# All three stages of a fused block written out without loops, and a layer's weights split partly one step early

## What is computed

```
x = x + ga * attention(norm(x), 16 heads of 8)                 # phase A, one sequence per item
h = norm(x); for i in range(6):                                # phase B, local attention, DEPTH = 6
    h = attn_layer(shift_tokens(h), Wqkv[i], ..., Wo[i]) + h   #   16 heads of 64, windows of 32 tokens
    h = ffn_layer(shift_tokens(h), ..., W1[i], W2[i]) + h      #   341 wide, gated by gelu
x = x + gb * h
x = x + ga * state_space(norm(x))                              # phase C, scan over the tokens
x = x + gb * (norm(x) @ W + low rank part)
```

## Time and profile before

| what | value |
|---|---|
| three timed runs | 4804.89, 4807.92 (median), 4809.58 us |
| the profiled execution | 4799.15 us |
| its span, first to last instruction | 4797.3 us |
| PE busy | 4226.0 us, 88% of the span |
| PE weight loads | 3150.4 us, 66% |
| DVE busy | 4007.1 us, 84% |
| ACT busy | 3749.9 us, 78% |
| POOL busy | 3518.3 us, 73% |
| phase A, about | 60 to 484 us |
| phase B, about | 484 to 4030 us |
| phase C, about | 4030 to 4797 us |
| mean granted clock of TensorE | 0.961 of 2.4 GHz |

### The profile page before, as it was taken

One profiled execution on the slowest core, in us unless ns is written; L12 is line 12 of the kernel. 1 busy time (PEld: TensorE's weight loads), 2 busy tenths in 40 slices (PEclk: granted clock), 3 DMA queues, 4 the chain that ended last, 5 costly groups with the idle time before them and its releaser, 6 DMA issues. The chain is left out here.

```text
span 4797.3 us, 131407 instructions
## 1 busy us (share of the span) xinstructions
PE 4226.0 (88%) x45166; PEld 3150.4 (66%) x45166; DVE 4007.1 (84%) x7658; ACT 3749.9 (78%) x11543; POOL 3518.3 (73%) x2504
## 2 busy tenths in 40 slices
PE   6988699998999989998889989999899998688887
PEld 3555477776777777776777767777677776354553
DVE  4776798888888888888888888898898895688887
ACT  2555588888888888888888888888888887677774
POOL 0100699988899888998989989899899995344444
PEclk9999799999999999999999999999999999788888
DMA  1000111111111111111111111111121111000000
GB/s 27 6 5 2 49 48 44 44 38 52 53 40 43 48 48 47 44 44 45 46 53 43 40 45 52 47 44 44 45 53 38 44 44 28 3 4 3 3 3 5
DMA packets 118641, 169.38 MB, mean 35 GB/s; under 512 B 26563, under 2 KB 44422, under 8 KB 118022
## 3 DMA queue, kind: packets, MB, share of 16 engines
q1 hardware_dynamic: 109246, 160.92, 12.7%
q10 hardware_dynamic: 8776, 0.45, 0.1%
HBM read 20.79 MB, written 2.10 MB: 5 GB/s over the span
## 5 line engine op out<-in xcount | busy, mean ns | idle before, releaser
L1377 POOL TENSOR_TENSOR b_w<-b_w,b_vt 128x512 f32<-128x512 f32 x768 | 1188.4, 1558 | 331.8 <-DVE b_vt L1289 184.1
L1381 POOL TENSOR_TENSOR b_rn<-b_ssm,all_neg_half 128x16 f32<-128x16 f32 x384 | 1171.7, 3051 | 32.0
L1174 ACT ACTIVATE b_Pr<-ps,b_nm 128x96 f32<-128x96 f32 x3072 | 1002.8, 353 | 3.4 <-DVE b_nm L1346 2.8
L1174 ACT ACTIVATION_READ_ACCUMULATOR b_Pr<-ps,b_nm 128x1 f32 x3072 | 677.1, 220 | 0.0
L1216 ACT ACTIVATE b_PT<-ps 96x512 f32<-96x512 f32 x768 | 458.1, 597 | 264.1 <-PE ps L1026 257.1
L1060 PE MATMUL ps<-b_Whi,b_xlo 128*128 128x512 f32 x1152 | 579.2, 503 | 61.7 <-DVE b_Wlo L1306 25.8
L989 PE MATMUL ps<-all_ident,b_w 128*128 128x128 f32 x3072 | 460.6, 281 | 182.3 <-DVE b_xtok L282 118.7
L1340 DVE TENSOR_TENSOR b_Pr<-b_Pr,b_rinv 128x384 f32<-128x384 f32 x768 | 547.0, 712 | 26.3
L1026 PE MATMUL ps<-all_ident,b_Pr 128*96 128x128 f32 x3072 | 479.2, 279 | 68.8 <-ACT b_PT L1216 47.1
L1287 DVE TENSOR_TENSOR b_w<-ps,until_b_rotab 128x512 f32<-128x512 f32 x768 | 524.0, 682 | 8.9 <-ACT b_sq L1193 5.4
L1346 DVE TENSOR_REDUCE b_nm<-ps 128x8 f32<-128x768 f32 x384 | 367.5, 957 | 190.8 <-PE ps L1015 184.6
(11 more groups left out here) (259 smaller groups left out, 9375.4 us busy)
## 6 DMA issues: line engine op xcount, KB each, us to landing
b_V<-b_Vraw SPq DMA_DIRECT2D x384, 192.0 KB, 2.6
b_V<-b_Vraw SPq DMA_DIRECT2D x384, 128.0 KB, 2.4
b_V<-b_Vraw SPq DMA_DIRECT2D x192, 64.0 KB
b_Wraw<-in_L_ffn_Wqkv SPq DMA_DIRECT2D x36, 256.0 KB, 3.4
b_Wo<-in_L_ffn_Wo SPq DMA_DIRECT2D x6, 512.0 KB, 4.5
a_xtok<-in_L_attn_hidden_states SPq DMA_DIRECT2D x16, 128.0 KB, 2.1
out<-c_xout SPq DMA_DIRECT2D x16, 128.0 KB, 1.8
b_W<-in_L_ffn_W SPq DMA_DIRECT2D x6, 341.0 KB, 3.3
```

Source lines behind the costliest of these rows:

```text
L1174: last = nc.scalar.activation(s.Pr[:, r % 2, j, i], ps[:, S_BANK[j], i * KEYS:(i + 1) * KEYS], ACT.Exp, bias=s.nm[:, r, j, i:i + 1], accum ...
L1377: nc.gpsimd.tensor_tensor(rows, rows, s.vt[:, i % 4], ALU.add).then_inc(s.pool_add, 1)
L1381: nc.gpsimd.tensor_tensor(s.rn[:, j], s.ssm[:, j], g.neg_half[:, 0:HB], ALU.pow).then_inc(s.pool_r, 1)
```

## The change

All steps of the three phases are written out with numbers; the three loops of the compute engines go. (SP keeps its own loops over the loads of phase A and the stores of phase C.) Since in phase B every step now knows its number, the step ahead of a layer's start can be told from the others (`last`): in it conversions 0 and 1 of the next layer are done, in slots 11 and 14, once the last pieces that read these columns are through. The `convert` step does the other four, in slots 1, 4, 7 and 10. At the very start (n = -1) conversions 0 and 1 stay in slot 0. The order of the last two chunks is swapped. SP's program for the loads of the raw weights isn't edited. The last two parts of the diff are ACT's and DVE's.

```
 def phase_a_steps(engine, body):
-    def whole(n):
+    for n in range(-2, NB + 2):
         body(StepA(n, n % 2, *[0 <= n + d < NB for d in (2, 1, 0, -1, -2)]))
-    for n in range(-2, 3):
-        whole(n)
-    with engine.Fori(1, NB // 2 - 2) as pair:
-        body(StepA(2 * pair + 1, 1, True, True, True, True, True))
-        body(StepA(2 * pair + 2, 0, True, True, True, True, True))
-    for n in range(NB - 3, NB + 2):
-        whole(n)
...
-CHUNKS = (0, 2, 4, 1, 5, 3)
-CONVERT_SLOT = {0: (0, 1), 4: (2,), 8: (3,), 10: (4,), 12: (5,)}
+CHUNKS = (0, 2, 4, 1, 3, 5)
+FIRST_SLOT = {0: (0, 1)}
+AHEAD_SLOT = {11: (0,), 14: (1,)}
+CONVERT_SLOT = {1: (2,), 4: (3,), 7: (4,), 10: (5,)}
...
+    def converted(self, slot):
+        pieces = []
+        if self.last:
+            pieces += [(self.front[0] + 1, k) for k in AHEAD_SLOT.get(slot, ())]
+        if self.convert:
+            if self.n == -1:
+                pieces += [(self.front[0], k) for k in FIRST_SLOT.get(slot, ())]
+            pieces += [(self.front[0], k) for k in CONVERT_SLOT.get(slot, ())]
+        return pieces
...
 def phase_b_steps(engine, body, between=None):
-    def whole(n):
+    for n in range(-1, ITEMS + 3):
         stages = stages_of(n)
         items = [divmod(n + d, NB) if there and n + d >= 0 else None for d, there in zip((1, 0, -1, -2, -3), stages)]
-        body(Step(n, n % 2, items[0], items[2], items[3], items[4], convert=n == -1))
...
-    with engine.Fori(0, DEPTH - 1) as l:
-        if between is not None:
-            between(l)
-        inner(l)
...
-    inner(DEPTH - 1)
-    for n in range(ITEMS - 1, ITEMS + 3):
-        whole(n)
+        layer, at = divmod(n, NB)
+        if between is not None and at == 3 and 0 <= layer < DEPTH - 1:
+            between(layer)
+        edge = at + 1 if 1 <= layer < DEPTH and at < 3 else None
+        body(Step(n, n % 2, items[0], items[2], items[3], items[4], convert=items[0] is not None and items[0][1] == 0, edge=edge,
+                  last=items[0] is not None and items[0][1] == NB - 1 and items[0][0] + 1 < DEPTH))
...
                 for slot in range(STEP_SLOTS):
-                    if step.convert:
-                        for k in CONVERT_SLOT.get(slot, ()):
-                            c = CHUNKS[k]
-                            act.wait_ge(s.wqkv_in[k % RAW], 16 * (WCHUNKS // RAW) * step.front[0] + 16 * (k // RAW) + 16)
-                            if k == 0:
-                                wait(act, s.proj_done, N_PIECES * f)
-                            nc.scalar.activation(s.Whi[:, c * 512:(c + 1) * 512], s.Wraw[:, k % RAW], ACT.Copy).then_inc(s.whi_done, 1)
+                    for layer, k in step.converted(slot):
+                        c = CHUNKS[k]
+                        act.wait_ge(s.wqkv_in[k % RAW], 16 * (WCHUNKS // RAW) * layer + 16 * (k // RAW) + 16)
+                        if step.last:
+                            act.wait_ge(s.proj_done, N_PIECES * f + max(PIECE.index(at) for at in PIECE if (QK_SLOT.get(at) or V_SLOT[at])[1] == c) + 1)
+                        else:
+                            wait(act, s.proj_done, N_PIECES * f)
+                        nc.scalar.activation(s.Whi[:, c * 512:(c + 1) * 512], s.Wraw[:, k % RAW], ACT.Copy).then_inc(s.whi_done, 1)
...
                 for slot in range(STEP_SLOTS):
-                    if step.convert:
-                        for k in CONVERT_SLOT.get(slot, ()):
-                            cols = slice(CHUNKS[k] * 512, (CHUNKS[k] + 1) * 512)
-                            dve.wait_ge(s.whi_done, WCHUNKS * lf + k + 1)
-                            nc.vector.tensor_tensor(s.Wlo[:, cols], s.Wraw[:, k % RAW], s.Whi[:, cols].bitcast(F32), ALU.subtract).then_inc(s.w_ready, 1)
+                    for layer, k in step.converted(slot):
+                        cols = slice(CHUNKS[k] * 512, (CHUNKS[k] + 1) * 512)
+                        dve.wait_ge(s.whi_done, WCHUNKS * layer + k + 1)
+                        nc.vector.tensor_tensor(s.Wlo[:, cols], s.Wraw[:, k % RAW], s.Whi[:, cols].bitcast(F32), ALU.subtract).then_inc(s.w_ready, 1)
```

More of the change, by code:

```diff
@@ L770, with __init__ @@
 class Step:
-    def __init__(self, n, odd, front, tail, ffn, closing, half=None, convert=False, edge=None):
+    def __init__(self, n, odd, front, tail, ffn, closing, half=None, convert=False, edge=None, last=False):
         self.n, self.odd, self.front, self.tail, self.ffn, self.closing, self.convert, self.edge = n, odd, front, tail, ffn, closing, convert, edge
+        self.last = last
         every = len(spare_uses(True, True, True, True, True))
@@ L809, in phase_b_steps @@
 def phase_b_steps(engine, body, between=None):
-    def whole(n):
+    for n in range(-1, ITEMS + 3):
         stages = stages_of(n)
         items = [divmod(n + d, NB) if there and n + d >= 0 else None for d, there in zip((1, 0, -1, -2, -3), stages)]
-        body(Step(n, n % 2, items[0], items[2], items[3], items[4], convert=n == -1))
[L815 to L821, removed]
-        whole(n)
-    with engine.Fori(0, DEPTH - 1) as l:
-        if between is not None:
-            between(l)
-        inner(l)
-        n, half = NB * l + NB - 1, NB // 2 * l + NB // 2 - 1
-        body(Step(n, 1, (l + 1, 0), (l, NB - 2), (l, NB - 3), (l, NB - 4), half, convert=True, edge=0))
-        body(Step(n + 1, 0, (l + 1, 1), (l, NB - 1), (l, NB - 2), (l, NB - 3), half + 1, edge=1))
-        body(Step(n + 2, 1, (l + 1, 2), (l + 1, 0), (l, NB - 1), (l, NB - 2), half + 1, edge=2))
-        body(Step(n + 3, 0, (l + 1, 3), (l + 1, 1), (l + 1, 0), (l, NB - 1), half + 2, edge=3))
-    inner(DEPTH - 1)
-    for n in range(ITEMS - 1, ITEMS + 3):
-        whole(n)
+        layer, at = divmod(n, NB)
[4 more added lines that the diff above has]
+                  last=items[0] is not None and items[0][1] == NB - 1 and items[0][0] + 1 < DEPTH))
 def phase_b(nc, g, d, ps):
@@ L1422, in phase_c_steps @@
 def phase_c_steps(engine, body):
-    def whole(n):
+    for n in range(-2, NB + 2):
         body(StepC(n, n % 2, *[0 <= n + d < NB for d in (2, 1, 0, -1, -2)]))
-    for n in range(-2, 2):
-        whole(n)
-    with engine.Fori(1, NB // 2 - 1) as pair:
-        for odd in range(2):
-            body(StepC(2 * pair + odd, odd, True, True, True, True, True))
-    for n in range(NB - 2, NB + 2):
-        whole(n)
 def phase_c(nc, g, d, ps, out):
```

## The result

The changed kernel takes 4822.57 us (median; 4816.53 to 4831.72) where the kernel before takes 4807.71 us (4803.02 to 4812.96) in the same runs: 1.0035 times as long, with a 95% interval of 1.0028 to 1.0043. It is slower by 14.9 us. The forecast was 4799.2 us, faster; the range (4779 to 4823) just holds the time, the sign is wrong.

What follows compares the result with a forecast made beforehand. Four engines 85 to 91% busy in local attention were taken to leave no slack for stalls, with losses at back edges and layer boundaries. -24.1 + 7.0 - 2.5 + 10.9 = -8.7 us gave a median of 4799.2 us, range 4779 to 4823.

Steps and rivals of the forecast that it cites:

- Part 1: Phase B's loop: four back edges go, each losing 6.03 us, and straight code costs nothing there; -24.1 us.
- Part 2: Constants replace registers: phase B's two steps 0.20 us longer, +7.0 us in all; phase C -2.5 us, phase A 0.
- Phase C: -2.5 us forecast: Phase C's steps: sequencer pieces of 0.03 us between waits go, 0.2 us in each of 12 steps; -2.5 us.
- Part 3: Five layer boundaries, weight conversions moved: 76.0 us lost instead of 65.1, +10.9 us, bounds -8.6 and +27.4.
- The sum of 15.2 us: Loss per layer boundary after the change, 0.5 + 0.7 + 11.3 + 2.2 + 0.5 us, bounds 11.3 and 18.5.
- the stall, put at 11.3 us: Slot 4 of each boundary: chunk 3's load stands behind V transfers, PE idle 11.62 us against 0.33; 11.3 us lost.
- 0.5 + 0.7 + 2.2 = 3.4 us: Conversions per boundary: 0.5 us for chunks 0 and 1 a step ahead, 0.7 for chunk 2, 2.2 for the last two.
- another 0.5 us for the clock: Each boundary: 0.5 us for the clock after 11.6 us of idle PE, mostly hidden by DVE; bounds 0 and 3.
- Slower: the long idle isn't hidden: Boundaries: idle PE costs 1.9 times its length, 21.5 us each, 4831 us in all; chance 0.13.
- The unrolled code stalls: Phase B: straight code pays the back edge's stall too, so no gain there; +15.4 us, 4823 us; chance 0.06.
- The early chunks pay: Boundaries: V transfers don't hold chunk 3's load back, 30 us instead of 76; -54.7 us, 4753 us; chance 0.08.
- Registers count for more: The 0.20 us don't spread beyond the last layer and phase C gains its upper bound; -18.2 us, 4789.7 us; chance 0.22.

Runs made afterwards that it cites:

- unroll_only: Kernel after, all three phases written out, but with the weight chunks' order and slots of the kernel before: 4789.35 us, 0.9967 of before.
- one_pass_loops: Kernel before with phase B's loop over layers written as four loops of one pass each, A and C looped: 4788.23 us, 0.9963 of before.
- after_a_looped: Kernel after with phase A's loop as before, B and C written out: 4812.73 us, 1.0022 of before.
- ac_straight_only: Kernel before with only phases A and C written out, phase B keeping its loop and slots: 4809.74 us, 1.0016 of before.
- b_straight_only: Kernel after with the loops of phases A and C as before, only phase B written out: 4811.64 us, 1.0010 of before.
- after_again: Kernel after, unchanged, measured once more in another set of runs: 4824.59 us, 1.0038 of before.
- early_loads: Kernel after, same slots, SP's loads of chunks 3 to 5 issued earlier so that none stands behind all V transfers: 4785.70 us, 0.9955 of before.
- after_8col: Kernel after with later layers' chunks converted in 8 columns only, late load of chunk 3 kept: 4799.51 us, 0.9987 of before.
- early_loads_8col: early_loads with later layers' chunks converted in their first 8 columns only, on ACT and DVE: 4752.93 us, 0.9888 of before.
- early_loads_none: early_loads with the conversions of all layers after the first left out, semaphores still counted up: 4726.03 us, 0.9837 of before.
- after_c_looped: Kernel after with phase C's loop as before, A and B written out: 4818.64 us, 1.0030 of before.
- spread_work: early_loads with A and C looped and five of six chunks converted in the last item's step, the sixth in slot 10: 4753.47 us, 0.9893 of before.

## Why the prediction was wrong, and where it was right

**Part 1 (back edges, -24.1 us).** Right: no "issue" wait of 3 us, no step of 40 us, unroll_only and one_pass_loops both some 17 us faster than before. One thing was left out: the kernel after has eight single steps that are 0.2 to 2.1 us longer than the rest (as 35.63, 37.71), 7.5 us in all where before, its back edges apart, has 0.6. They aren't a price of straight code as such, since after_a_looped has none; in a written-out B most of them come with phase A's form.

**Part 2 (registers).** Right for phase B: the pace of 71.56 us in every layer, +7.0 us forecast and +6.5 in the traces, wherever the constants are. Why fewer instructions give a longer pair, no run tells. Phase C: -2.5 us forecast, but its steps didn't change (40.96 us). The pieces of 0.03 us in the earlier trace rows lay beside other work. A and C together went the other way, by 6.8 us in ac_straight_only and up to 12 us between b_straight_only and after. Part of that is the single long steps of phase B and its dearer back edges; what makes them stays open. In the timed runs unroll_only (A and C written out) is only 1 us slower than one_pass_loops (both looped), so the price isn't a fixed term.

**Part 3 (boundaries, +10.9 us).** Here the forecast failed: +31.3 us (96.4 - 65.1), above the upper bound of 27.4; with after_again's 92.6 us it is still +27.5. This is 20.4 us more than forecast, the largest part of the miss. The mechanism was right and its rows nearly to the letter: ACT's wait 9.19 us (9.7 forecast), values to chunk 3 at ACT 6.14 us (7.21), the chain behind it 4.42 us (4.41), PE idle 10.55 us (11.62). The sum of 15.2 us was built of the wrong terms:
- the stall, put at 11.3 us, costs 6.8 to 7.6 us (after and after_again less early_loads) to 9.2 us (after_8col less early_loads_8col), since without it PE still waits 2.88 us at the same place;
- the six conversions, put at 0.5 + 0.7 + 2.2 = 3.4 us, with another 0.5 us for the clock, cost 11.1 us without any stall (early_loads less early_loads_none). This is the mis-sized term and the step of the forecast that failed.

The error was to add up what PE visibly waited for. The same method applied to before gives 2.31 + 1.91 us of a mean loss of 65.1 / 5 = 13.0 us: two thirds had no row, and I didn't ask what they were. The six pairs take 6 x (0.62 + 0.69) = 7.9 us of ACT and DVE, and 11.1 us is more than that. That engines which are 85 to 91% busy pass such work on to the end, with small waits that no view ranks high, fits these numbers, but no run shows it wait by wait. (A slip without effect: the raw chunks 0 to 2 are loaded at the layer's fourth step and not by its third.)

**The rivals.** "Slower: the long idle isn't hidden" named 18.9 us a boundary as the point from which the kernel is over 0.2% slower, and the boundary came to 19.3. But its reason is refuted: a microsecond of idle PE cost 1.0 us (0.9 to 1.2 over the pairs of kernels above), not 1.9. From 3 us into the gap to 2.7 us beyond it the clock is at 0.50, 1.2 GHz, as the Trainium skill, in "TensorE: Matmul & The Clock Gate", section on HAM oscillation, warns that it will; but in these 10.2 us PE was busy only 2.74 us, and waited the rest anyway. "The unrolled code stalls" gave 4823 us, nearly the time measured, by a mechanism that isn't there: no straight step shows an "issue" wait of 3 us where the back edge was, and unroll_only is faster than before. "The early chunks pay" fell: SP's order is as read, and without its wait (early_loads) the time is 4786 and not 4753 us, because the conversions cost more than the rival's 6 us. "Registers count for more" fell too, the pace being the slower one everywhere.

The rule of the Trainium skill, "Runtime: NRT & Kernel Launch", section on instruction fetch mechanics, holds for the jumps of phase B, whose body is large; for the loop of C the trace shows no such stall, for A and C written out no run shows a gain, and the ratios of ac_straight_only, after_a_looped, after_c_looped and b_straight_only lean to a small loss.

## What to carry to other kernels

Before an itemised forecast is trusted, itemise the kernel before by the same rule: where the visible waits explain a third of a known loss, the missing term will be missing in the forecast as well. A conversion brought forward past the arrival of its load loses more than it gains; follow every operand of a moved instruction back to the issue of its DMA and to what stands ahead of that issue. And where engines are over 85% busy, try to move work into another step: here other slots of the same step brought a boundary to between 11.7 and 12.9 us, and five of six chunks in the step before to 6.5, though not every chunk moved brought something.

## What the runs showed of the hardware that I had not expected

The same subtraction on DVE takes 0.68 us in one place and 1.76 us in another. In spread_work the long one starts at 2808.82, while a POOL instruction runs from 2808.75 to 2810.04, and ends 0.54 us behind it; the short ones at 2791.34 and 2812.30 start before POOL's. With 8 columns instead of 512 (the 30 of early_loads_8col) it takes 0.15 to 0.17 us 15 times and 0.81 to 0.88 us 15 times. Each long one starts while a POOL operation on 128x512 runs and ends within 0.03 us of that one's end:

```profile
2809.69 2.93 POOL L1377 TENSOR_TENSOR b_rn<-b_ssm,all_neg_half 128x16 f32<-128x16 f32 x1
2812.41 0.17 DVE L1302 TENSOR_TENSOR b_Wlo<-b_Wraw,b_Whi 128x8 fp32r<-128x8 f32 x1 [0.82 <-ACT b_Whi L1181]
...
2813.86 1.28 POOL L1373 TENSOR_TENSOR b_w<-b_w,b_vt 128x512 f32<-128x512 f32 x1 [1.24 <-DVE b_vt L1285]
2814.29 0.88 DVE L1302 TENSOR_TENSOR b_Wlo<-b_Wraw,b_Whi 128x8 fp32r<-128x8 f32 x1
```

In after a DVE instruction that takes 0.29 us 92 times takes 1.90 us once at each boundary (2874.90 above), beside one of POOL that runs from 2874.65 to 2876.64. No experiment took POOL's instruction away, so this is read from the traces and not shown. The Trainium skill, "SBUF — State Buffer", section on SBUF's two separate sides, says that DVE, in an operation with two SBUF inputs among others, and GpSimd share a port pair that one of them holds for its whole instruction while the other waits; the long ones agree. But ten of the short ones run their 0.17 us inside a POOL operation of 2.93 us on 128x16 (b_rn) and aren't held up. They lie in its first or last 0.5 us, and POOL's times are rough, so these ten neither agree nor refute. An estimate from these rows is 0.7 us for each of the three small subtractions a boundary that are held up, 2.0 us of the 4.8 us that six small conversions cost by their mere presence; what makes the rest is open.

The program's form also reaches into code that wasn't edited: with A and C written out and B's loop kept, B's four back edges cost 31.1 us instead of 24.1 (one profiled execution each), and with B written out it is the single long steps that come with A's form. Why is open.
